# A two-layer graph attention kernel: the cosine threshold made from norms that go through DRAM, without matmuls

## The chip, the core and the metric

The kernel runs on one core of one Trainium2 chip. Its engines each follow a list of instructions in order: TensorE (PE; PEld is its weight load), VectorE (DVE), ScalarE (ACT), GpSimd (POOL) and SyncE (SP, which here only issues DMAs). They meet through semaphores. The metric is the device time of one execution in microseconds (us), the median of several runs; less is better.

## The reference, cut to what matters

128 graphs of 128 nodes with 512 features go through two attention layers. The change touches one line of layer 0: which pairs of nodes have a cosine above 0.1.

```python
def _L0_gnn_ref(embs, score_mask, map_w, map_b, q_w, q_b, k_w, k_b, gcn_map_w, gcn_map_b, gcn_W):
    # embs = relu(layernorm(x)); 8 heads of dk = 64
    m = embs @ map_w.T + map_b
    sem = m.reshape(b, s, h, dk).transpose(0, 2, 1, 3)
    norm = jnp.maximum(jnp.linalg.norm(sem, axis=-1, keepdims=True), COS_EPS)
    n = sem / norm
    cos = jnp.einsum('bhsd,bhtd->bhst', n, n)
    cos = cos * (~sm).astype(cos.dtype)
    cos_adj = (cos > THRESHOLD).astype(embs.dtype)
    q, k = split(m @ q_w.T + q_b), split(m @ k_w.T + k_b)
    scores = jnp.where(sm, NEG, q @ k.T / sqrt(dk))
    p_attn = jax.nn.softmax(scores, axis=-1) * keep
    adj = cos_adj * p_attn
    Ax = adj @ split(embs @ gcn_map_w.T + gcn_map_b)
    return relu((Ax @ gcn_W.T) / (adj.sum(-1, keepdims=True) + 1.0))
# x = x + layer 0; then x = x + layer 1 (softmax attention, 4 heads of 64, masked by adj, output projection)
```

The kernel doesn't divide by the norms. It compares the product of two rows with 0.1 times the product of their norms: m_s . m_t - 0.1 |m_s| |m_t| > 0, for 8 heads of 128x128 pairs in each graph.

## The kernel before, in words

Every product runs on TensorE in float16 with each operand split into an upper and a lower part (`hi`, `lo`; three passes). ACT makes the upper parts (a copy to float16), POOL or DVE the lower ones (original minus upper), and DMA transposes bring them into the layout that the next product needs.

The graphs go through a software pipeline of slots, one for each graph, written out in full. In slot n an engine works on graph n (scores, cosines, softmax and gate of layer 0), on graphs n+1 to n+6 (loads, layer norm, the products m, q, k, v; these for two graphs at once) and on graphs n-1 to n-5 (weighted sums, layer 1, result). **Even and odd slots differ**: q, k and the norms of a pair of graphs are made in odd slots, m and v in even ones. Each engine has its own `slot(s)` function with the calls in the order in which they are issued. Nothing reorders them afterwards; a stage that waits holds up all that stands behind it on its engine. The first slots (preparation of weights, graphs 0 to 2) and the last three (`late_slots`) have orders of their own.

PSUM holds `s_ps` (scores, 2 banks), `c_ps` (cosines, 2 banks) and four banks of `unit_ps` that a table (`UNITS`) gives to products in turn. TensorE may start a unit only when DVE has emptied the last product in that bank. In odd slots bank 3 goes from `o1o` (the sums of layer 1, emptied by `o1_rows(s, 4)`, L1389 and L1391) to `lq` (L1886), and DVE reaches `o1_rows(s, 4)` only after `gate(s)` (L1280).

The threshold before, for a pair of graphs, in the odd slot ahead of them:

1. PE `norms` (L1980) sums the squares; DVE `norm_sums` (L1400) takes them out, times 0.1; POOL `norm_rows` takes the root with a power of 0.5 (L781) and makes float16 upper and lower parts (L786, L788) in `norm_parts`.
2. SP `turn_norms` (L558) transposes them with two DMAs into `norm_t`.
3. DVE `threshold_rows` (L1414) multiplies them by a mask of heads into `norm_r`.
4. PE `cosines` (L1942) adds minus the product of the norms to the cosines in `c_ps`: two matmuls of 64 rows by 512 columns for each graph.

After that `gate` (L1280) keeps those of the exponentials whose `c_ps` is above 0. The exponentials are ACT's (`scores_exp`, L949 and eight L939), the maximum before them DVE's (L1274), the masking DVE's (L1264).

## Time and profile before

| | |
|---|---|
| median of 3 runs | 2512.72 us (2511.32 to 2512.87) |
| profiled execution | 2513.7 us, its span 2511.9 us |
| PE / PEld / DVE / ACT / POOL busy | 99% / 79% / 81% / 69% / 82% |
| granted TensorE clock, mean | 0.997 |
| DMA engines busy | 59.8% (data queue) |

The profile is one execution. "Busy" is the share of the span in which an engine had an instruction running; a matmul's end is modelled. The span leaves out 1.8 us around the program. A wait is shown as idle time in front of an instruction, with the one that released it.

### The profile page before, as it was taken

The numbers are of one execution on the slowest core, as the hardware profiler recorded it, in microseconds if no ns is written. First come the engines' busy times: TensorE is split into PE (matmuls) and PEld (weight loads), VectorE is DVE, ScalarE is ACT, GpSimd is POOL, SyncE is SP. The second block draws the span as 40 slices with busy tenths as digits, with TensorE's granted clock in tenths as the row PEclk, the third lists the DMA queues.
The fourth block names the chain that finished last, engine by engine and source line by source line (L and its number), as shares of the span: only waits on it lengthen the run. The fifth ranks groups of instructions, "written<-read, shape, count | busy, mean of one in ns | idle before, by whom it ended". The sixth has DMA issues, their size and how long they took to land.

```text
span 2511.9 us, 77339 instructions
## 1 busy us (share of the span) xinstructions
PE 2474.3 (99%) x29880; PEld 1978.8 (79%) x29880; DVE 2028.9 (81%) x3426; ACT 1737.7 (69%) x4528; POOL 2064.2 (82%) x2330
## 2 busy tenths in 40 slices
PE   8899999999999999999999999999999999999997
PEld 6677878878878778778788788788787787787775
DVE  6888788788788888888887887888878888888876
ACT  5676676676776766766766766767767667667666
POOL 4788888888888888888888888888888888888875
PEclk9999999999999999999999999999999999999999
DMA  5456665656656656665656566556566666566652
GB/s 154 92 117 120 121 124 115 128 115 124 128 114 123 130 116 118 130 117 120 121 117 126 116 122 127 118 123 128 115 123 129 117 118 126 116 123 121 120 100 75
DMA packets 840557, 300.56 MB, mean 120 GB/s; under 512 B 782464, under 2 KB 790144, under 8 KB 840192
## 3 DMA queue, kind: packets, MB, share of 16 engines
q1 hardware_dynamic: 840192, 295.62, 59.8%
q8 instruction: 238, 3.90, 0.7%
q14 instruction: 127, 1.04, 0.1%
HBM read 75.80 MB, written 33.55 MB: 44 GB/s over the span
## 4 chain that ended last, share of the span: by engine, by line
PE 93%; DVE 2%; ACT 1%; POOL 1%; issue 1%; DMA 1%; SPq 0%; POOLq 0%; DVEq 0%; ACTq 0%
PE unit_ps L1886 26%; PE unit_ps L2064 26%; PE unit_ps L1900 25%; PE s_ps L1910 4%; PE s_ps L1969 4%; PE c_ps L1910 3%; PE unit_ps L2036 2%; PE unit_ps L1910 2%; PE c_ps L1942 1%; PE unit_ps L1980 1%; ACT e_ec L939 0%; DVE e_ec L1280 0%; POOL norm L781 0%; DMA e_ec<-in_L_gnn_q_w_dram 0%; DMA norm_t<-norm_parts 0%
## 5 line engine op out<-in xcount | busy, mean ns | idle before, releaser
L939 ACT ACTIVATE e_ec<-e_ec,neg_mx 128x128 f32<-128x128 f32 x1008 | 390.0, 388 | 4.1
L2064 PE MATMUL unit_ps<-m_hl,w_q_hi 128*128 128x256 f16 x2048 | 358.2, 274 | 0.0
L2064 PE MATMUL unit_ps<-m_hl,w_k_hi 128*128 128x256 f16 x2048 | 355.6, 272 | 0.6 <-DVE qk_sb L1316 0.6
L1035 ACT ACTIVATE qk_hl<-qk_sb 128x512 f16<-128x512 f32 x256 | 153.3, 622 | 283.2 <-DVE qk_sb L1316 283.2
L1886 PE MATMUL unit_ps<-h_t,w_m_hi 128*128 128x256 f16 x2048 | 342.4, 274 | 2.4 <-issue 1.3
L1900 PE MATMUL unit_ps<-w_v_hi,h_t 128*128 128x512 f16 x1024 | 325.1, 379 | 0.0
L996 ACT ACTIVATE h_sb<-x,shift,rstd 128x512 f32<-128x512 f32 x128 | 104.1, 813 | 281.3 <-POOL shift L809 281.3
L1886 PE MATMUL unit_ps<-h_t,w_m_lo 128*128 128x256 f16 x1024 | 280.5, 274 | 0.0
L734 POOL TENSOR_TENSOR e_ec<-e_ec 128x1024 f16<-128x1024 f32 x126 | 269.1, 2136 | 3.3 <-ACT e_ec L969 2.1
L1280 DVE SCALAR_TENSOR_TENSOR e_ec<-c_ps,e_ec 128x1024 f32<-128x1024 f32 x126 | 154.2, 1224 | 118.5 <-ACT e_ec L939 118.5
L2064 PE MATMUL unit_ps<-m_hl,w_q_lo 128*128 128x256 f16 x1024 | 238.6, 273 | 0.0
L2064 PE MATMUL unit_ps<-m_hl,w_k_lo 128*128 128x256 f16 x1024 | 237.3, 272 | 0.0
L2064 PEld LDWEIGHTS unit_ps<-m_hl,w_q_hi 128*128 128x128 f16 x2048 | 200.7, 98 | 39.1 <-issue 16.8
L1886 PEld LDWEIGHTS unit_ps<-h_t,w_m_hi 128*128 128x128 f16 x2048 | 196.0, 98 | 31.9 <-issue 2.8
L2064 PEld LDWEIGHTS unit_ps<-m_hl,w_k_hi 128*128 128x128 f16 x2048 | 200.1, 98 | 23.2 <-issue 0.6
L729 POOL TENSOR_TENSOR p_hl<-p_sb,p_hl 128x512 f16<-128x512 f32 x128 | 148.6, 1161 | 79.9 <-ACT p_hl L962 79.9
L710 POOL TENSOR_TENSOR h_hl<-h_sb,h_hl 128x512 f16<-128x512 f32 x128 | 148.5, 1160 | 67.0 <-ACT h_hl L1004 67.0
L1900 PE MATMUL unit_ps<-w_v_lo,h_t 128*128 128x512 f16 x512 | 194.0, 379 | 0.0
L1900 PEld LDWEIGHTS unit_ps<-w_v_hi,h_t 128*128 128x128 f16 x1024 | 100.2, 98 | 114.1 <-issue 0.3
L1316 DVE SCALAR_TENSOR_TENSOR qk_sb<-unit_ps,qk_factor,col_qb 128x512 f32<-128x512 f32 x128 | 96.1, 751 | 116.2 <-PE unit_ps L2064 115.4
L939 ACT ACTIVATION_READ_ACCUMULATOR e_ec<-e_ec,neg_mx 128x1 f32 x1008 | 188.3, 187 | 0.0
L781 POOL TENSOR_TENSOR norm<-sq_sum,plus_half 128x16 f32<-128x16 f32 x64 | 187.1, 2923 | 1.4 <-DVE sq_sum L1400 1.3
(280 smaller groups left out, 7550.8 us busy)
## 6 DMA issues: line engine op xcount, KB each, us to landing
xa<-in_x_dram SPq DMA_DIRECT2D x128, 256.0 KB, 3.3
x<-in_x_dram SPq DMA_DIRECT2D x128, 256.0 KB, 2.9
out_dram<-x SPq DMA_DIRECT2D x128, 256.0 KB, 2.4
h_t<-h_hl SPq DMA_TRANSPOSE x254, 3.3
ec_t<-e_ec SPq DMA_TRANSPOSE x252, 3.2
adj_in<-in_adj_dram SPq DMA_DIRECT2D x128, 16.0 KB, 2.0
norm_t<-norm_parts SPq DMA_TRANSPOSE x128, 2.3
p_t<-p_hl SPq DMA_TRANSPOSE x126, 3.3
```

The source lines that it names most:

```text
L710: nc.gpsimd.tensor_tensor(h1_hl[:, a, 1, :], h1_sb[:, a, :], h1_hl[:, a, 0, :], ALU.subtract).then_inc(h1_lo, 1)
L729: nc.gpsimd.tensor_tensor(p1_hl[:, b, 1], p1_sb[:, b], p1_hl[:, b, 0], ALU.subtract).then_inc(p1_lo, 1)
L734: nc.gpsimd.tensor_tensor(e_hl[:, 1], e_of(s), e_hl[:, 0], ALU.subtract).then_inc(e_lo, 1)
L781: nc.gpsimd.tensor_tensor(norm[:, :], sq_sum[:, :], plus_half[:, :], ALU.pow).then_inc(norm_done, 1)
L939: ins = nc.scalar.activation(e[:, h, :], e[:, h, :], ACT.Exp, bias=neg[:, h:h + 1], scale=SCALE, accum_out=sums[:, h:h + 1])
L996: nc.scalar.activation(h1_sb[:, a, :], x1[:, (s.n - 1) % 8, :], ACT.Relu, bias=shift1[:, 0:1], scale=rstd1[:, 0:1]).then_inc(h1_done, 1)
L1035: nc.scalar.activation(dst[:, 0, c, :], src[:, c, :], ACT.Copy).then_inc(done, 1)
L1280: nc.vector.scalar_tensor_tensor(out=e_of(s), in0=c_ps[:, :, :].rearrange("p a (b n) -> p (a b) n", b=4), scalar=0.0, in1=e_of(s), op0=ALU ...
L1886: ins = nc.tensor.matmul(out, w[a][:, i, c * P:(c + 1) * P], h[:, :, b, i, :], start=n == 0, stop=n == len(passes) - 1)
L1900: ins = nc.tensor.matmul(ps, h[:, a, i, :], w[b][:, i, :], start=n == 0, stop=n == len(passes) - 1)
L1910: ins = nc.tensor.matmul(outs[half][c], st[r, a, c, cols], mv[r, b, c, cols], start=n == 0 and (last or c == 0), stop=last and n == 2)
L2064: ins = nc.tensor.matmul(ps[:, c % 2 * 2 * P:(c % 2 + 1) * 2 * P], w[a][:, i, c * P:(c + 1) * P], parts[:, b, i, :], start=n == 0, stop=n ...
```

## The change

The threshold is made without TensorE:

- POOL `norm_rows` keeps only the power of 0.5; L786, L788, `norm_parts`, `norm_t`, `norm_r` and the mask are gone.
- SP `keep_norms` stores the norms of both graphs of a pair to DRAM (128 nodes x 2 x 8 float32, pieces of 32 bytes), and `spread_norms`, once that has landed, loads each graph's 128x8 norms into all 128 partitions (`norm_n`, 4 KB in each partition, 512 KB for a graph).
- ACT `threshold` makes `least[s, h, t]` = norm of t (from `norm_n`, read with a step of 8 float32) times 0.1-scaled norm of s (one value for each partition), with eight copies of 128 columns for each graph. `least` has one buffer.
- DVE `above` subtracts `least` from the cosines in PSUM, one operation of 1024 columns for each graph; `gate` waits for it.
- The last graph's `least` is POOL's (`last_threshold`).

```diff
--- before.py
+++ after.py
@@ sync
+            def keep_norms(s):
+                if s.has(1):
+                    sp.wait_ge(norm_done, s.at(lambda t: (t + 1) // 2 + 1))
+                    for g in range(2):
+                        wait(sp, norm_in[g], s.at(lambda t: 16 * ((t + 1) // 2)))
+                    sp.dma_start(norm_d.rearrange("g n h -> n g h"),
+                                 norm[:, :].rearrange("p (g h) -> p g h", g=2)).then_inc(norm_kept, 16)
+            def spread_norms(s):
+                if s.has(1):
+                    wait(sp, threshold_done, s.at(lambda t: t + 1))
+                    sp.wait_ge(norm_kept, s.at(lambda t: 16 * ((t + 1) // 2 + 1)))
+                    for g in range(2):
+                        sp.dma_start(norm_n[:, g].rearrange("p n h -> p (n h)"),
+                                     norm_d[g].rearrange("(a n) h -> a (n h)", a=1).broadcast_to([P, P * H])).then_inc(norm_in[g], 16)
@@ gpsimd, norm_rows
+                    wait(pool, norm_kept, s.at(lambda t: 16 * ((t + 1) // 2)))
+                    wait(pool, threshold_done, s.at(lambda t: t + 1))
                     nc.gpsimd.tensor_tensor(norm[:, :], sq_sum[:, :], plus_half[:, :], ALU.pow).then_inc(norm_done, 1)
-                    ... (copy and subtract into norm_parts)
@@ scalar
+            def threshold(s):
+                if s.has(0):
+                    g = s.n % 2
+                    act.wait_ge(norm_in[g], s.at(lambda t: 16 * (t // 2 + 1)))
+                    act.wait_ge(norm_done, s.at(lambda t: t // 2 + 1))
+                    wait(act, lowered, s.at(lambda t: t))
+                    for h in range(H):
+                        ins = nc.scalar.activation(least[:, h, :], norm_n[:, g, :, h], ACT.Copy, scale=norm[:, g * H + h:g * H + h + 1])
+                    ins.then_inc(threshold_done, 1)
@@ scalar, even slots
+                    threshold(s)
                     scores_exp(s)
@@
                     lv_upper(s)
+                    threshold(Slot(s.n + 1, None, B))
                     h1_rows(s)
@@ vector
+            def above(s):
+                if s.has(0):
+                    dve.wait_ge(c_full, s.at(lambda t: t + 1))
+                    dve.wait_ge(threshold_done, s.at(lambda t: t + 1))
+                    cosine = c_ps[:, :, :].rearrange("p a (b n) -> p (a b) n", b=4)
+                    nc.vector.tensor_tensor(cosine, cosine, least[:, :, :], ALU.subtract).then_inc(lowered, 1)
             def gate(s):
                 if s.has(0):
                     dve.wait_ge(e_done, s.at(lambda t: t + 1))
-                    dve.wait_ge(c_full, s.at(lambda t: t + 1))
+                    dve.wait_ge(lowered, s.at(lambda t: t + 1))
@@ vector, odd slots
                     q_features(s, 0)
                     o1_rows(s, 5)
+                    above(s)
                     q_features(s, 1)
@@
-                    threshold_rows(s)
@@ vector, even slots
                     l1_mask(s, 3)
+                    above(s)
                     gate(s)
@@ tensor, cosines
                     row_pairs([[c_ps[:, a, c * P:(c + 1) * P] for c in range(C)] for a in range(2)], parts, parts,
-                              columns(s.n % 2), last=False)
-                    pe.wait_ge(threshold_done, s.at(lambda t: t // 2 + 1))
-                    for a in range(2):
-                        r = slice(a * DK, (a + 1) * DK)
-                        ins = nc.tensor.matmul(c_ps[:, a, :], norm_t[r, 0, :], norm_r[r, s.n % 2].rearrange("p c n -> p (c n)"),
-                                               start=False, stop=True)
-                    ins.then_inc(c_full, 1)
+                              columns(s.n % 2)).then_inc(c_full, 1)
```

Three places, in the steady part of the program. First ACT, where an even slot begins, before:

```order
L996 ACTIVATE h_sb<-x,shift,rstd 128x512 [waits h1_lo,ln1_step]
L1004 ACTIVATE h_hl<-h_sb 128x512 [waits h1_in,h1_done]
L949 ACTIVATE neg_mx<-mx 128x8 [waits mx_done,den_done]
L939 ACTIVATE e_ec,row_sum<-e_ec,neg_mx 128x128 [waits neg_mx_done]
L939 ACTIVATE e_ec,row_sum<-e_ec,neg_mx 128x128 x7
```

and with the change:

```order
L1007 ACTIVATE h_sb<-x,shift,rstd 128x512 [waits h1_lo,ln1_step]
L1015 ACTIVATE h_hl<-h_sb 128x512 [waits h1_in,h1_done]
L951 ACTIVATE least<-norm_n,norm 128x128 [waits lowered,norm_done,norm_in0]
L951 ACTIVATE least<-norm_n,norm 128x128 x7
L960 ACTIVATE neg_mx<-mx 128x8 [waits mx_done,den_done]
L940 ACTIVATE e_ec,row_sum<-e_ec,neg_mx 128x128 [waits neg_mx_done]
L940 ACTIVATE e_ec,row_sum<-e_ec,neg_mx 128x128 x7
```

The eight products for the even graph stand between layer 1's rows of the slot before (`h_sb`, `h_hl`) and the even graph's exponentials (`e_ec`), and wait for `norm_in0`. Further on in the same even slot, ACT before:

```order
L976 ACTIVATE v_sb<-v_rows_sb 128x8x64 [waits av_full,unit_out1]
L987 ACTIVATE lv_sb<-unit_ps,v_scale 128x8x64 [waits unit_full]
L996 ACTIVATE h_sb<-x,shift,rstd 128x512 [waits h1_lo,ln1_step]
L1004 ACTIVATE h_hl<-h_sb 128x512 [waits h1_in,h1_done]
L976 ACTIVATE v_sb<-v_rows_sb 128x8x64 [waits av_full,unit_out3]
```

and with the change:

```order
L987 ACTIVATE v_sb<-v_rows_sb 128x8x64 [waits av_full,unit_out1]
L998 ACTIVATE lv_sb<-unit_ps,v_scale 128x8x64 [waits unit_full]
L951 ACTIVATE least<-norm_n,norm 128x128 [waits lowered,norm_done,norm_in1]
L951 ACTIVATE least<-norm_n,norm 128x128 x7
L1007 ACTIVATE h_sb<-x,shift,rstd 128x512 [waits h1_lo,ln1_step]
L1015 ACTIVATE h_hl<-h_sb 128x512 [waits h1_in,h1_done]
L987 ACTIVATE v_sb<-v_rows_sb 128x8x64 [waits av_full,unit_out3]
```

The eight products for the odd graph stand behind `lv_sb` and ahead of layer 1's rows, so ahead of the odd graph's exponentials too. Third, SP in an odd slot, before:

```order
L516 DMA_TRANSPOSE o_t<-o_hl 128x4x128 [waits unit_full,o1_lo]
L548 DMA_TRANSPOSE ec_t<-e_ec 128x8x128 [waits av_full,e_hi]
L558 DMA_TRANSPOSE norm_t<-norm_parts 128x1x128 [waits c_full,norm_split]
L558 DMA_TRANSPOSE norm_t<-norm_parts 128x1x128
L548 DMA_TRANSPOSE ec_t<-e_ec 128x8x128 [waits av_full,e_lo]
L584 DMA out_dram<-x 128x512 [waits unit_out3]
```

and with the change:

```order
L516 DMA_TRANSPOSE o_t<-o_hl 128x4x128 [waits unit_full,o1_lo]
L548 DMA_TRANSPOSE ec_t<-e_ec 128x8x128 [waits av_full,e_hi]
L558 DMA norm_d<-norm 128x2x8 [waits norm_in1,norm_in0,norm_done]
L568 DMA norm_n<-norm_d 128x1024 [waits norm_kept,threshold_done]
L568 DMA norm_n<-norm_d 128x1024
L548 DMA_TRANSPOSE ec_t<-e_ec 128x8x128 [waits av_full,e_lo]
L595 DMA out_dram<-x 128x512 [waits unit_out3]
```

One store and two loads of 512 KB stand where two small transposes stood, ahead of the transpose of the lower half of `ec_t`, and SP waits for the store to land (`norm_kept`) in front of the loads.

## Rows read from the trace of the kernel before

**Rows 1.** Page, part 1: busy us (share) and instructions of each engine.
```profile
PE 2474.3 (99%) x29880; PEld 1978.8 (79%) x29880; DVE 2028.9 (81%) x3426; ACT 1737.7 (69%) x4528; POOL 2064.2 (82%) x2330
```

**Rows 2.** Waits, whole run: waiter, releaser, us in total, times, longest us.
```profile
ACT h_sb L996 <- POOL shift L809: 281.3, 127, 3.4
...
DVE e_ec L1280 <- ACT e_ec L939: 118.5, 123, 2.2
...
PE unit_ps L1886 <- DVE o_sb L1391: 0.4, 1, 0.4
```

**Rows 3.** Chain of work, 1206 to 1246: start us, us, what.
```profile
1208.48 0.21 PE c_ps L1942 x2
...
1218.52 2.62 PE unit_ps L1886 x24
```

**Rows 4.** Timeline of ACT, 1199 to 1256: start us, us, instruction, [idle before].
```profile
1208.27 0.81 ACT L996 ACTIVATE h_sb<-x,shift,rstd 128x512 f32<-128x512 f32 x1 [2.00 <-POOL shift L809]
...
1215.94 0.40 ACT L1027 ACTIVATE o_hl<-o_sb 128x256 f16<-128x256 f32 x1
...
1229.25 0.81 ACT L996 ACTIVATE h_sb<-x,shift,rstd 128x512 f32<-128x512 f32 x1 [2.15 <-POOL shift L809]
1230.09 0.63 ACT L1004 ACTIVATE h_hl<-h_sb 128x512 f16<-128x512 f32 x1
1231.98 0.21 ACT L949 ACTIVATE neg_mx<-mx 128x8 f32<-128x8 f32 x1 [1.26 <-DVE mx L1274]
...
1235.54 1.28 ACT L937 ACTIVATE p_sb<-p_sb,neg_lmx 128x128 f32<-128x128 f32 x4
...
1243.24 0.61 ACT L976 ACTIVATE v_sb<-v_rows_sb 128x512 f16<-128x512 f32 x1
1243.76 0.67 ACT L987 ACTIVATE lv_sb<-unit_ps,v_scale 128x512 f16<-128x512 f32 x1
1246.43 0.81 ACT L996 ACTIVATE h_sb<-x,shift,rstd 128x512 f32<-128x512 f32 x1 [2.00 <-POOL shift L809]
```

**Rows 5.** Timeline of POOL, the same stretch.
```profile
1206.21 0.23 POOL L805 TENSOR_SCALAR nm<-mv 128x1 f32<-128x1 f32 x1
...
1218.16 2.90 POOL L781 TENSOR_TENSOR norm<-sq_sum,plus_half 128x16 f32<-128x16 f32 x1
...
1222.03 1.15 POOL L755 TENSOR_TENSOR qk_hl<-qk_sb,qk_hl 128x512 f16<-128x512 f32 x1
...
1227.18 1.09 POOL L805 TENSOR_SCALAR nm<-mv 128x1 f32<-128x1 f32 x1
```

**Rows 6.** Timeline of DVE, the same stretch.
```profile
1214.51 0.75 DVE L1316 SCALAR_TENSOR_TENSOR qk_sb<-unit_ps,qk_factor,col_qb 128x512 f32<-128x512 f32 x1 [1.69 <-PE unit_ps L2064]
1216.06 1.22 DVE L1280 SCALAR_TENSOR_TENSOR e_ec<-c_ps,e_ec 128x1024 f32<-128x1024 f32 x1 [0.80 <-ACT e_ec L939]
...
1217.41 0.42 DVE L1391 TENSOR_TENSOR o_sb<-unit_ps,inv_lsum 128x256 f32<-128x256 f32 x1
...
1226.98 1.21 DVE L1414 TENSOR_TENSOR norm_r<-norm_t,norm_mask 128x1024 f16<-128x1024 f16 x1
```

**Rows 7.** DMA issues: times, KB each, median us from issue to landing.
```profile
x<-in_x_dram SPq DMA_DIRECT2D x128, 256.0 KB, 2.9
...
norm_t<-norm_parts SPq DMA_TRANSPOSE x128, 2.3
...
p_sb<-in_L_gnn_Wv_dram SPq DMA_DIRECT2D x1, 512.0 KB, 7.2
bias_o<-in_L_gnn_bo_dram SPq DMA_DIRECT2D x1, 256.0 KB, 7.3
```

**Rows 8.** Stretches: busy us by engine, PEclk, DMA share, GB/s (last).
```profile
24.00:28.00 4.00, 3.99 (x34) 3.64 (x35) 4.00 (x8) 4.00 (x6) 0.00 (x0) 1.00 1.08 338
...
1222.00:1230.00 8.00, 8.00 (x122) 6.44 (x120) 6.15 (x7) 2.07 (x3) 7.51 (x9) 1.00 0.30 59
```

**Rows 9.** Timeline of ACT, first slot.
```profile
62.40 0.19 ACT L949 ACTIVATE neg_mx<-mx 128x8 f32<-128x8 f32 x1
```

More of the change, by code:

```diff
@@ L282, in build @@
         ec_t = sb("ec_t", [P, 2, H, P], F16)
-        norm_parts = sb("norm_parts", [P, P + 2 * H], F16)
-        norm_t = sb("norm_t", [P, 2, P], F16)
-        norm_r = sb("norm_r", [P, 2, C, P], F16)
-        norm_mask = sb("norm_mask", [P, 2 * C])
+        norm_d = nc.dram_tensor("norm_d", (2, P, H), F32).ap()
+        norm_n = sb("norm_n", [P, 2, P, H])
+        least = sb("least", [P, H, P])
         ident16 = sb("ident16", [P, P], F16)
@@ L395, in build @@
         norm_done = sem("norm_done")
-        norm_split = sem("norm_split")
-        norm_in = sem("norm_in")
+        norm_kept = sem("norm_kept")
+        norm_in = [sem(f"norm_in{i}") for i in range(2)]
         threshold_done = sem("threshold_done")
+        lowered = sem("lowered")
         masked = sem("masked")
@@ L643, in _ @@
             turn_e(z, 0, e_hi)
-            turn_norms(z)
+            keep_norms(z)
+            spread_norms(z)
             turn_e(z, 1, e_lo)
@@ L1092, in slot @@
                     squares(s)
+                    threshold(s)
                     scores_exp(s)
@@ L1095, in slot @@
                     v_upper(s, "va", 2)
+                    threshold(Slot(s.n + 1, None, B))
                     h1_rows(s)
@@ L1099, in slot @@
                 else:
+                    threshold(s)
                     scores_exp(s)
@@ L1107, in slot @@
                     lv_upper(s)
+                    threshold(Slot(s.n + 1, None, B))
                     h1_rows(s)
@@ L1202, in _ @@
             lqk_upper(z, "lq", lq_hl, LQ)
+            threshold(a)
             scores_exp(a)
@@ L1535, in slot @@
                     l1_mask(s, 3)
+                    above(s)
                     gate(s)
@@ L1756, in _ @@
             o1_rows(z, 5)
+            above(z)
             q_features(z, 1)
@@ L1766, in _ @@
             x1_stats(z)
-            threshold_rows(z)
             lqk_lower(z, "lq", lq_hl, LQ, 0)
             scores_mask(a)
+            above(a)
             scores_mask(b)
@@ L1774, in _ @@
             x1_stats(a)
+            above(b)
             gate(b)
@@ L1902, in rows, with row_pairs @@
                 return ins
-            def row_pairs(outs, mv, st, cols, last=True):
+            def row_pairs(outs, mv, st, cols):
                 for c in range(len(outs[0])):
@@ L1910, in row_pairs @@
                             ins = nc.tensor.matmul(outs[half][c], st[r, a, c, cols], mv[r, b, c, cols],
-                                                   start=n == 0 and (last or c == 0), stop=last and n == 2)
+                                                   start=n == 0, stop=n == 2)
                 return ins
@@ L1977, in norms @@
                     for g in range(2):
-                        out = ps[:, 0:2 * H].rearrange("p (a g c) -> p g a c", a=2, g=2)[:, g]
+                        out = ps[:, 0:2 * H].rearrange("p (g a c) -> p g a c", a=2, g=2)[:, g]
                         for n, (c, part) in enumerate((c, part) for c in range(C) for part in range(2)):
```

53 lines of the change are left out of this document (13 added, 40 removed).

## The prediction

> **What bounds the kernel now.** I read the page's busy shares first. TensorE is busy 99% of the span, but the other four are at 69% to 82% [rows 1], so one engine made slower could take over. Then the waits of the whole run: TensorE hardly waits for anyone. The longest that bears on the change is ACT, which waits 281 us in all for POOL's layer norm of layer 1, and DVE's gate waits 118 us for ACT's exponentials [rows 2]. Those waits are slack, and the question is who uses it up. Last the chain of work and the timelines of one pair of graphs (an odd and an even slot). Layer 1's rows in ACT (L996) start at 1208.27 and again at 1246.43: a pair takes 38.16 us [rows 4]. There are 64 pairs, and about 61 of them run at this pace; the first and last 70 to 110 us are different.
>
> **TensorE.** The two threshold matmuls of a graph are 0.21 us of the chain [rows 3], since both halves of the array run at once (the groups show 0.38 us for each matmul, but they overlap). Two graphs: 0.43 us a pair, so TensorE alone would need 37.73 us. Over 61 pairs that is -26 us. Nothing else in TensorE changes.
>
> **Where a delay would reach TensorE.** In odd slots unit `lq` starts at 1218.52 in the bank that `o1_rows(s, 4)` empties; that ends at 1217.41 + 0.42 = 1217.83 and stands behind the gate, which starts when the odd graph's exponentials are done [rows 3, 6]. So 0.7 us less the semaphore, about 0.5 us, is all that the odd exponentials may be late against TensorE. Only one such wait is in the trace, of 0.4 us [rows 2].
>
> **The round through ACT and POOL.** The odd exponentials end (L1027 starts) at 1215.94; then POOL's power at 1218.16, its `q` lower part at 1222.03, the rest of POOL's slot up to shift L809, which releases ACT's L996 at 1229.25, L1004, exponentials from 1231.98, the ACT work up to L987, L996 at 1246.43, and the next odd exponentials [rows 4, 5]. I step through it with the change:
>
> - POOL loses L786 and L788: the power ends at 1221.06, and the lower part of `q`, which started at 1222.03, follows at 1221.10. -0.93 us.
> - POOL's L805 took 1.09 us, from 1227.18 to 1228.27, beside L1414 of DVE, from 1226.98 to 1228.19 [rows 5, 6]. The same operation with no such neighbour takes 0.23 us [rows 5], so I count L1414's going as -0.86 us. Bounds: 0 (something else takes its place) and -1.2 us (L804 before it goes faster too). The two make 1.79 us, ACT's L996 starts at 1227.46, and ACT is free 0.84 + 0.54 us later, at 1228.84.
> - The even graph's eight products. No ACT copy of 128 columns stands in the trace. The nearest is L937, 128 columns with one value per partition, contiguous: four in 1.28 us with the first 0.39, so 0.297 us for each further one [rows 4]. Eight: 2.38 us. Bounds: below, no less than this pitch, since a shape as short is mostly fixed cost; above, 0.40 each, if every column takes twice the 0.82 ns that I get from 0.61 us for 512 and 0.39 us for 128 less their fixed part: 3.2 us. I take 2.38. ACT is done at 1231.22, and the even exponentials start there instead of 1231.98: 0.76 us early, as the maximum (DVE, relieved of L1414) is ready by then.
> - From L949 to the end of L987 nothing changes. L987 starts 1243.76 and its follower could have started 0.09 before its end (as 1243.24 + 0.61 and 1243.76 show), at 1244.34 [rows 4]. Early by 0.76: 1243.58. The odd graph's products: 2.38, so 1245.96, where L996 had waited until 1246.43 for POOL. 0.47 us early; what was 2.00 us of idle is full.
>
> So the round would take 38.16 - 0.47 = 37.69 us, and TensorE 37.73 us. **They tie.** The cover that hides 4.8 us of new ACT work a pair is spent to the last tenth; any shift of POOL's or ACT's pieces (the bounds above are -0.3 to +0.9 us on the POOL side) shows in the time if it is late and not if it is early. I put 0.15 us a pair on that: +9 us over 61 pairs.
>
> **DVE.** L1414 goes (1.21 us in this pair); two subtractions come. The gate has their shape and operands (1024 columns, one operand in PSUM, one in SBUF): 1.22 us [rows 6]. Plus 1.2 us a pair, and both lie in waits: in odd slots ahead of `q_features(s, 1)`, where DVE sat 1.69 us for TensorE; in even slots ahead of the gate, where it sits for ACT's exponentials (118.5 us over 123 times, 1 us each [rows 2]). Cost 0; if the cover is gone, 0.2 us for a graph in even slots (1.2 against 1.0).
>
> **SP and DMA.** The store can go when the power ends, 1221.06. No store of 32-byte pieces is in the trace; the nearest small transfer lands after 2.3 us [rows 7]. Bounds 2 and 5 us. Then 512 KB: 256 KB of x land after 2.9 us, and another 256 KB at the 338 GB/s of the weight loads is 0.8 us [rows 7, 8]: 3.7. Together with issue the even graph's norms are there at about 1227.4, and ACT wants them at 1228.84. That the source is the same 4 KB for all partitions costs nothing that I can see: the broadcast bias took 7.3 us where its neighbour in the queue took 7.2 [rows 7]. The engines are 30% busy from 1222 to 1230 [rows 8], so there is room. The lower half of `ec_t`, now behind 1 MB, lands near 1231 instead of 1229; TensorE needs it at 1235. Cost 0.
>
> **Ends of the program.** In slot 0 ACT is the chain: its exponentials start at 62.40 straight behind other work [rows 9]; the first eight products go in front of them, +2.4 us, and those of graph 1 stand in front of graph 1's; DVE's L1414 is gone there. I take +4 us (0 to 5). At the end the norms were on the chain already; a store and a load (6 us) take the place of two POOL operations, a transpose and L1414 (about 7), against two subtractions and POOL's last product: +1 us.
>
> **The sum** against the profiled execution: -26 + 9 + 4 + 1 = -12 us, span 2511.9 to 2500, execution 2513.7 to 2501.5. The median of the runs is 1 us under the profiled one: 2500.5 us.
>
> **Rivals.** *The strided read.* `threshold` reads `norm_n` with a step of 32 bytes, and no ACT operation of the trace reads SBUF with such a step. If each column then takes twice as long, eight products take 3.2 us: +0.84 twice a pair. The round is 39.4 us, TensorE waits for bank 3 in every odd slot, and 1.2 us over 61 pairs is +74, +10 at the ends with 8 more products there: 2597 us. This is the case on the other side. For it: the step is new. Against: short operations are mostly fixed cost. 0.27.
>
> The Trainium skill ("SBUF — State Buffer", section "Door 1: The DMA port swizzle (why `[64,N]` ≈ `[32,N]`)") speaks for this rival: engines read 16-byte lines, and "how far you can stride for free depends on dtype: 4 fp32"; here the step is 8. No row of this case shows it.
>
> *Norms late.* If the store takes 5 us and the load 4, ACT has the even norms at 1230.1 at best, 1.3 us after it is free: round 39.0 us, +0.8 us a pair against before, +49 and +5 at the ends: 2567 us. For it: 256 pieces of 32 bytes, at a time when the queue is full up to 1222. Against: the small rows of [rows 7]. 0.13. The Trainium skill ("DMA: Bandwidth & Descriptors", section "Specifications") has pieces under 512 bytes done as read-modify-write, which would lengthen this store; no run here shows it.
>
> *All hidden.* POOL gains the whole 1.2 us, the round is shorter than TensorE's 37.73, and the gain is -26 + 3: 2490 us. 0.14.
>
> **Chances.** The forecast 0.46, its own range 2488 to 2525 us (0.33 of it under 2507.7, 0.08 within 5 us of before, 0.05 above). About 0.2%, 5 us, is what a measurement tells from no change. Faster 0.14 + 0.33 = 0.47, same 0.08, slower 0.05 + 0.27 + 0.13 = 0.45. The range that leaves out 2 in 10 runs from the all-hidden case to about the middle of the strided one: 2487 to 2598.
>
> **What would show it.** ACT's products at 0.30 us apart (0.40: the strided rival). Their first one in even slots with no wait for a DMA (a wait for `norm_n`: norms late). ACT's 281 us wait for POOL nearly gone; POOL's L805 back at 0.23. TensorE waiting for `o_sb` in front of `lq`, in few pairs and for tenths, if they tie; in each pair for over 0.5 us, if I am wrong on the round. A pair at 37.7 to 37.9 us. The forecast falls if TensorE waits elsewhere, as for `ec_t` or the end of the cosines.

## The result and the profile after

The changed kernel takes 2642.38 us (median of 4 runs, 2641.85 to 2643.54) against 2512.23 us before: ratio 1.0515, 95% interval 1.0502 to 1.0529. It is 130 us slower, where I forecast 12 us faster, and 44 us above the end of my range. The profiled span went from 2511.9 to 2640.8 us.

Page, part 1, of the changed kernel (busy us, share, instructions; before: [rows 1]):

```profile
PE 2484.8 (94%) x29624; PEld 1981.5 (75%) x29624; DVE 2131.1 (81%) x3490; ACT 2147.2 (81%) x5544; POOL 1981.2 (75%) x2195
```

TensorE's busy time grew by 10 us though 256 matmuls are gone (part of the run is at a lower granted clock, below); its share fell to 94%. ACT grew by 410 us. The chain of work that ended last (page, part 4), by engine, first before and then with the change:

```profile
PE 93%; DVE 2%; ACT 1%; POOL 1%; issue 1%; DMA 1%; SPq 0%; POOLq 0%; DVEq 0%; ACTq 0%
```

```profile
ACT 53%; issue 21%; POOL 15%; PE 8%; DVE 2%; DMA 1%; ACTq 0%; SPq 0%; POOLq 0%; DVEq 0%
```

TensorE was the bound and is no longer. The waits of the whole run answer to [rows 2] (waiter, releaser, us, times, longest):

```profile
DVE e_ec L1305 <- ACT e_ec L940: 235.7, 109, 3.5
...
PE unit_ps L1903 <- DVE o_sb L1416: 105.4, 60, 2.1
...
ACT h_sb L1007 <- POOL shift L809: 57.1, 49, 3.0
```

ACT no longer waits for POOL for 281 us. The gate waits twice as long for ACT, and TensorE now waits in nearly every pair for the bank that `o1_rows(s, 4)` empties behind the gate (L1903 is what L1886 was, L1416 what L1391 was, L1007 what L996 was). The timeline of ACT, one pair (answers to [rows 4]; from the L1007 of one odd slot to that of the next 39.96 us, where 38.16 stood from one even slot to the next):

```profile
1293.53 0.81 ACT L1007 ACTIVATE h_sb<-x,shift,rstd 128x512 f32<-128x512 f32 x1 [1.08 <-POOL shift L809]
1294.38 0.63 ACT L1015 ACTIVATE h_hl<-h_sb 128x512 f16<-128x512 f32 x1
1294.91 3.45 ACT L951 ACTIVATE least<-norm_n,norm 128x128 f32<-128x128 f32 x8
1298.27 0.19 ACT L960 ACTIVATE neg_mx<-mx 128x8 f32<-128x8 f32 x1
...
1310.04 0.67 ACT L998 ACTIVATE lv_sb<-unit_ps,v_scale 128x512 f16<-128x512 f32 x1
1310.61 3.44 ACT L951 ACTIVATE least<-norm_n,norm 128x128 f32<-128x128 f32 x8
1313.95 0.80 ACT L1007 ACTIVATE h_sb<-x,shift,rstd 128x512 f32<-128x512 f32 x1
...
1321.61 0.40 ACT L1038 ACTIVATE o_hl<-o_sb 128x256 f16<-128x256 f32 x1
...
1333.49 0.82 ACT L1007 ACTIVATE h_sb<-x,shift,rstd 128x512 f32<-128x512 f32 x1 [1.09 <-POOL shift L809]
```

Both blocks of eight stand without a gap in front and behind: ACT is full from 1293.53 to 1321.61. A block holds ACT for 3.36 us (from 1294.91 to 1298.27) or 3.34 us (from 1310.61 to 1313.95), and I had 2.38. The groups (busy us, mean ns, idle before):

```profile
L951 ACT ACTIVATE least<-norm_n,norm 128x128 f32<-128x128 f32 x1016 | 437.9, 515 | 3.0 <-DMA norm_n<-norm_d 3.0
```

A product takes 0.515 us and starts 0.42 us after the last one (from 3.45 - 0.51 over 7). Its idle time for a DMA is 3.0 us in the whole run, once.

POOL in the odd slot (answers to [rows 5]) and TensorE at the bank:

```profile
1323.83 2.90 POOL L782 TENSOR_TENSOR norm<-sq_sum,plus_half 128x16 f32<-128x16 f32 x1
1326.71 1.15 POOL L754 TENSOR_TENSOR qk_hl<-qk_sb,qk_hl 128x512 f16<-128x512 f32 x1
1327.82 2.57 POOL L733 TENSOR_TENSOR e_ec<-e_ec 128x1024 f16<-128x1024 f32 x1
...
1332.30 0.23 POOL L805 TENSOR_SCALAR nm<-mv 128x1 f32<-128x1 f32 x1
```

```profile
1323.65 0.38 PE L1903 MATMUL unit_ps<-h_t,w_lq_hi 128*128 128x256 f16 x2 [2.07 <-DVE o_sb L1416]
```

L805 is at 0.23 us as forecast, but that shows little: before, it took about 1.1 us in only 14 of its 128 executions, and one of them was the pair that I had read. The lower half of `e_ec` (L733), 2.13 us in the same stretch before, takes 2.57; before it had the row

```profile
1223.15 2.13 POOL L734 TENSOR_TENSOR e_ec<-e_ec 128x1024 f16<-128x1024 f32 x1
```

The starts of L1007 over the whole run give the pairs: of 60 steady ones 44 take about 39.95 us and 16 about 40.43, mean 40.08 (before 37.9 to 38.5, mean 38.15). 60 x 1.93 = 116 us; the first and last slots are 13 us longer. That is the 129 us of the span.

### The profile page after: what moved, and what is told of

Its sections match the earlier page's. It is cut to its first block, busy times and chain, and to the rows that moved or that the text cites. A ratio compares the mean times of both kernels' runs of the same rounds, so it can differ in the third digit from the quotient of the medians.

```text
span 2640.8 us, 78086 instructions
## 1 busy us (share of the span) xinstructions
PE 2484.8 (94%) x29624; PEld 1981.5 (75%) x29624; DVE 2131.1 (81%) x3490; ACT 2147.2 (81%) x5544; POOL 1981.2 (75%) x2195
## 4 chain that ended last, share of the span: by engine, by line
ACT 53%; issue 21%; POOL 15%; PE 8%; DVE 2%; DMA 1%; ACTq 0%; SPq 0%; POOLq 0%; DVEq 0%
ACT least L951 15%; ACT e_ec L940 13%; PE unit_ps L1903 5%; ACT p_sb L938 5%; POOL e_ec L733 4%; POOL qk_hl L754 4%; ACT h_sb L1007 4%; ACT v_sb L987 3%; ACT e_ec L980 2%; ACT m_hl L1064 2%; POOL x L715 2%; PE unit_ps L2075 2%; ACT h_hl L1027 2%; ACT xa L1022 2%; ACT sq_hl L1054 2%
## 5 line engine op out<-in xcount | busy, mean ns | idle before, releaser
L951 ACT ACTIVATE least<-norm_n,norm 128x128 f32<-128x128 f32 x1016 | 437.9, 515 | 3.0 <-DMA norm_n<-norm_d 3.0
L1903 PE MATMUL unit_ps<-h_t,w_m_hi 128*128 128x256 f16 x2048 | 341.2, 274 | 4.1 <-DVE qk_sb L1341 3.1
L733 POOL TENSOR_TENSOR e_ec<-e_ec 128x1024 f16<-128x1024 f32 x126 | 296.6, 2354 | 11.4 <-ACT e_ec L980 8.8
L1903 PE MATMUL unit_ps<-h_t,w_lq_hi 128*128 128x256 f16 x1024 | 197.0, 297 | 106.5 <-DVE o_sb L1416 105.4
L1903 PE MATMUL unit_ps<-h_t,w_m_lo 128*128 128x256 f16 x1024 | 279.9, 273 | 0.0
L1903 PEld LDWEIGHTS unit_ps<-h_t,w_m_hi 128*128 128x128 f16 x2048 | 195.8, 98 | 33.0 <-issue 4.4
L1365 DVE TENSOR_TENSOR qk_hl<-qk_sb,qk_hl 128x512 f16<-128x512 f32 x128 | 180.6, 1411 | 45.8 <-ACT qk_hl L1046 45.8
L1903 PEld LDWEIGHTS unit_ps<-h_t,w_lq_hi 128*128 128x128 f16 x1024 | 104.9, 106 | 140.8 <-issue 120.5
```

What stands on the lines that cost most here:

```text
L733: nc.gpsimd.tensor_tensor(e_hl[:, 1], e_of(s), e_hl[:, 0], ALU.subtract).then_inc(e_lo, 1)
L951: ins = nc.scalar.activation(least[:, h, :], norm_n[:, g, :, h], ACT.Copy, scale=norm[:, g * H + h:g * H + h + 1])
L1365: nc.vector.tensor_tensor(k_hl[:, 1, c, :], k_sb[:, c, :], k_hl[:, 0, c, :], ALU.subtract).then_inc(k_lo, 1)
L1903: ins = nc.tensor.matmul(out, w[a][:, i, c * P:(c + 1) * P], h[:, :, b, i, :], start=n == 0, stop=n == len(passes) - 1)
```

## The experiments

Each stands against runs of the kernel before on the same chip. The cuts of code are shortened (`...`). "Pair" is the distance of L1007 (L996) from one odd slot to the next, the commonest value of the profiled execution.

### e1: the products read contiguously

```diff
-ins = nc.scalar.activation(least[:, h, :], norm_n[:, g, :, h], ACT.Copy, scale=...)
+ins = nc.scalar.activation(least[:, h, :], norm_n[:, g].rearrange("p n h -> p (n h)")[:, h * P:(h + 1) * P], ACT.Copy, scale=...)
```

> The changed kernel, but ScalarE's products read 128 contiguous values of norm_n instead of every eighth one (so they take the norms of the wrong nodes; everything else, the store and the loads too, is as in the changed kernel). Theory A, the step: a product took 0.42 us from one to the next (3.36 us for eight) because of the 32-byte step; contiguous it takes the 0.30 us of the exponentials of 128 columns, eight take 2.4 us, the round through ScalarE and GpSimd is 2 us a pair shorter, and the time is 2510 to 2525 us. Theory B, the products themselves or the DMA traffic beside them are slow (a copy with one factor per partition, 1 MB of loads per pair): the pitch stays near 0.42 us and the time near 2640 us.

Measured: 2505.93 us, ratio to before 0.9972 (0.9961 to 0.9984), pair 37.93 us.

```profile
L951 ACT ACTIVATE least<-norm_n,norm 128x128 f32<-128x128 f32 x1016 | 309.0, 387 | 3.0 <-DMA norm_n<-norm_d 3.0
```

The same operation takes 515 ns in the changed kernel and 387 here, with the same loads running beside it; eight take 2.43 us. Theory A holds: 136 us hang on the step of one read. It came out below my 2510 to 2525, 5 us above the 2500.5 us of the forecast.

### e2, e5, e3: the step in between, with a layout that is right

The norms are stored and spread in blocks of W heads: W = 4 (step of 16 bytes, e2), 2 (8 bytes, e5), 1 (contiguous, e3).

```diff
-norm_n = sb("norm_n", [P, 2, P, H])
+norm_n = sb("norm_n", [P, 2, H // W, P, W])
-sp.dma_start(norm_d.rearrange("g n h -> n g h"), ...)
+sp.dma_start(norm_d.rearrange("g c n w -> n (g c) w"), ...)
-nc.scalar.activation(least[:, h, :], norm_n[:, g, :, h], ...)
+nc.scalar.activation(least[:, h, :], norm_n[:, g, h // W, :, h % W], ...)
```

> The changed kernel with the norms stored and spread as 2 blocks of 4 heads: pieces of 16 bytes in the store, ScalarE reads norm_n with a step of 16 bytes. It computes the same as the changed kernel. Theory A as the Trainium skill has it (page 'SBUF — State Buffer', a step of 4 float32 is free): pitch 0.30 us, as contiguous, 2510 to 2525 us. If the cost grows with the step: pitch between 0.30 and 0.42, about 0.36 us, eight take 2.9 us and the time is about 2575 us. Theory B: 0.42 us and 2640 us. If the 512 pieces of the store land later than the 128 to 256 of before, ScalarE waits for norm_n.

> The changed kernel with the norms stored and spread as 4 blocks of 2 heads: ScalarE reads norm_n with a step of 8 bytes; the store has 1024 pieces of 8 bytes. It computes the same as the changed kernel. Steps of 16 and of 32 bytes gave the same pitch of 0.42 us for 128 columns and a step of 4 bytes 0.30 us. If any step but the contiguous one costs this, the pitch is 0.42 us again and the store on top makes ScalarE wait for norm_n (the 2048 pieces of 4 bytes landed too late by 7.6 us a pair): 2700 us or more. If a step of 8 bytes is still free, the pitch is 0.30 us. The pitch is what this run is for; its time depends on the store.

> The changed kernel with the norms stored head by head: pieces of 4 bytes, 2048 of them in the store, and a contiguous read in ScalarE. It computes the same as the changed kernel. Theory A: pitch 0.30 us, and if the store lands in under about 5 us, 2510 to 2525 us; if the small pieces take longer (8 us or more), ScalarE waits for norm_n in even slots for 3 us or more a pair and the time is 2600 us or above. Theory B: pitch 0.42 us, 2640 us.

Measured: e2 2644.47 us (ratio 1.0524, 1.0508 to 1.0540), e5 2598.02 (1.0345, 1.0331 to 1.0359), e3 2955.52 (1.1765, 1.1745 to 1.1786). The groups of e2, e5, e3:

```profile
L951 ACT ACTIVATE least<-norm_n,norm 128x128 f32<-128x128 f32 x1016 | 437.2, 515 | 3.3 <-DMA norm_n<-norm_d 3.1
```

```profile
L951 ACT ACTIVATE least<-norm_n,norm 128x128 f32<-128x128 f32 x1016 | 319.0, 398 | 80.4 <-DMA norm_n<-norm_d 80.4
```

```profile
L951 ACT ACTIVATE least<-norm_n,norm 128x128 f32<-128x128 f32 x1016 | 309.7, 388 | 441.6 <-DMA norm_n<-norm_d 441.6
```

16 bytes cost exactly what 32 do; e2's time is the one that I had named for theory B, but e1 has ruled that theory out. 8 bytes are nearly free (398 against 387 ns). The price has moved into the store: its rows (times, KB, median us to landing) in the changed kernel, e2 and e5 are

```profile
norm_d<-norm SPq DMA_DIRECT2D x64, 8.0 KB, 1.9
```

```profile
norm_d<-norm SPq DMA_DIRECT2D x64, 8.0 KB, 2.8
```

```profile
norm_d<-norm SPq DMA_DIRECT2D x64, 8.0 KB, 4.7
```

for the same 8 KB in 256, 512 and 1024 pieces; with 2048 pieces ACT waited 441.6 us for the loads behind it. With 32-byte pieces the store lands just under my range of 2 to 5 us. The Trainium skill (page "DMA: Bandwidth & Descriptors", section "Specifications"), cited in the prediction for read-modify-write under 512 bytes, let me expect a longer store; at 1.9 us, under the 2.3 us that I took, none shows. No run has pieces of 512 bytes or more to compare.

### e4: one product instead of eight

```diff
-for h in range(H):
+for h in range(1):
     ins = nc.scalar.activation(least[:, h, :], ...)
```

The other seven heads' parts of `least` are set to 0 once, at the start.

> The changed kernel with one product of 128 columns for each graph instead of eight (the other seven heads keep a threshold of 0); all waits, the store, the loads and the subtraction stay. If ScalarE's time is the whole loss and nothing else of the change costs: the round through ScalarE and GpSimd is 2 x 2.9 = 5.9 us shorter than in the changed kernel, TensorE is the bound at 37.73 us a pair and the time is 2488 to 2495 us. If DMA (waits for norm_n, a late ec_t) or VectorE's subtraction costs something of its own, it is above 2500 us.

Measured: 2485.54 us (ratio 0.9891, 0.9876 to 0.9905), pair 37.70 us, 2.5 us below the range I gave. The loads, the store, the waits and the subtraction, all still there, cost nothing as long as TensorE is the bound. TensorE alone needs 37.70 us a pair; the prediction had 37.73.

### e6: contiguous for the even graph alone

```diff
+norm_n[:, g, :, h] if g else norm_n[:, g].rearrange("p n h -> p (n h)")[:, h * P:(h + 1) * P]
```

> The changed kernel, ScalarE's products contiguous for the even graph of a pair alone (with the norms of the wrong nodes), strided for the odd one. If both blocks of eight stand on one round whose pieces add up: half of what the contiguous read gave, less what lies below TensorE's own pace: the changed kernel takes about 40.1 us a pair, so this one 39.1 us, and 2575 to 2585 us. If only one of the two blocks is on the path, the time is near 2506 or near 2642 us.

Measured: 2569.15 us (1.0222, 1.0207 to 1.0238), a little under 2575. Pairs: 37.93 (e1), 38.93 (e6), 39.95 us (changed kernel). Each block of eight adds 1.0 us, which is 3.45 - 2.43 = 1.02 of the block itself. Both blocks are on one round, and it adds.

### e10: one POOL operation out of the round

```diff
@@ gpsimd, odd slots
                     e_lower(s)
-                    result_base(s)
                     norm_l1(s)
+                    result_base(s)
```

> The changed kernel with one move: in odd slots GpSimd makes layer 1's layer norm (norm_l1) ahead of result_base (L715, 1.27 us), which stood in front of it. It computes the same. If the round odd exponentials - GpSimd - ScalarE L1007 - exponentials is the bound: up to 1.3 us of it go, but ScalarE reaches L1007 only after the lk part (L1072), which TensorE's late lq holds: in the trace of the changed kernel that leaves 0 to 1.1 us a pair, on the mean about 0.5: 2600 to 2620 us. If the round is not what bounds it: 2642 us.

Measured: 2575.03 us (1.0239, 1.0225 to 1.0253), pair 38.76 us: 67 us faster with the strided read in place. More than expected: I had read ACT's slack from a pair of 40.43 us, in which L1007 does not wait for POOL; in most pairs it waits 1.1 us. So the round through POOL was the bound, and nearly all of L715's 1.27 us came back (39.95 - 38.76 = 1.2 us). What holds e10 at 38.76 us, still 1 us above TensorE's pace, is a second round (see e14 and e17).

### e15: e1's contiguous read and e10's move together

> The contiguous read (the norms of the wrong nodes, as in e1) with result_base behind norm_l1. The round is 36.9 us, TensorE bounds at 37.73: 2483 to 2490 us, against 2506 of e1. If the 20 us that e1 lay above the run with one product came from somewhere else than the round (DMA, VectorE's subtraction): 2506 us stays.

Measured: 2491.32 us (0.9920, 0.9906 to 0.9935), pair 37.70: TensorE's own pace. The 15 us between this and e1 are the tie that the forecast priced at 9 us (0.15 a pair; it was 0.23).

### e7, e9: what the matmuls are worth in the kernel before

e7 cuts the threshold matmuls to 8 columns, e9 the product with the mask too (both leave the threshold out for all other columns):

```diff
@@ e7 and e9, tensor
-nc.tensor.matmul(c_ps[:, a, :], norm_t[r, 0, :], norm_r[r, s.n % 2].rearrange("p c n -> p (c n)"), ...)
+nc.tensor.matmul(c_ps[:, a, 0:8], norm_t[r, 0, :], norm_r[r, s.n % 2].rearrange("p c n -> p (c n)")[:, 0:8], ...)
@@ e9, vector, threshold_rows
-nc.vector.tensor_tensor(norm_r[:, :, :, :]...)
+nc.vector.tensor_tensor(norm_r[:, :, 0, 0:8], ...)
```

> The kernel before, with its two threshold matmuls of a graph (L1942) cut from 512 to 8 columns; norms, transposes, the products with the mask and all waits stay (the threshold is left out for all but 8 columns). My step: 0.21 us a graph of TensorE's chain, 0.43 us a pair, -26 us: 2486 to 2489 us, since before these the round through ScalarE and GpSimd had 2 us of slack. If TensorE was not the bound or the round is as long: 2505 us or more.

> The kernel before with eight columns in its threshold matmuls (L1942), as the run before, and with the product with the mask (L1414) cut to the same eight columns (the threshold is left out for all others). Theory P: TensorE lost 0.28 us a pair in the run before because layer 1's scores (L1910) wait for the lower part of lk (L1365), which stands behind L1414 on VectorE, and lq for the gate; without L1414 the wait for lk is gone, and the time is 2486 to 2495 us. Theory Q: another bound (the round through GpSimd with L786 and L788, or the clock) holds the kernel at 2506 us whatever L1414 takes.

Measured: e7 2506.28 us (0.9974, 0.9963 to 0.9985), pair 38.00; e9 2485.82 (0.9887, 0.9873 to 0.9900), pair 37.74. The matmuls alone give 6 us, not 26. The timeline of VectorE in e7 shows who held TensorE:

```profile
1259.59 2.29 DVE L1414 TENSOR_TENSOR norm_r<-norm_t,norm_mask 128x1024 f16<-128x1024 f16 x1
1261.80 0.74 DVE L1365 SCALAR_TENSOR_TENSOR lk_hl<-unit_ps,unscale,lk_hl 128x512 f16<-128x512 f32 x1
```

and its chain of work at the same place:

```profile
1261.80 0.75 DVE lk_hl L1365
1262.55 0.05 issue
1262.59 0.84 PE unit_ps L1910 x24
```

L1414 stands in front of L1365, and layer 1's scores (L1910) need L1365. It is so in the whole run: in 62 of 64 pairs of e7 L1910 starts 0.06 us after L1365 ends. This was the next bound behind the matmuls, and with L1414 gone too (e9, theory P) the time is about 20 us less. The change takes both away, so the sum of the prediction (-26) was right for the change and its account was not. L786 and L788, which e9 keeps, were worth nothing there.

The trace of the kernel before had already shown how near this bound was:

```profile
PEld unit_ps L1910 <- DVE lk_hl L1365: 4.0, 12, 0.9
```

In 12 of 64 pairs the weight loads of L1910 waited for L1365, and over all pairs L1910 started only 0.24 us (median) after L1365's end. Of the 0.43 us a pair that the matmuls take, less than 0.2 could be gained.

### e8, e16: products and subtraction as one VectorE operation

```diff
-    nc.vector.tensor_tensor(cosine, cosine, least[:, :, :], ALU.subtract)
+    for h in range(H):
+        nc.vector.scalar_tensor_tensor(out=cosine_h, in0=norm_n[:, g, :, h], scalar=norm_s_h, in1=cosine_h, op0=ALU.mult, op1=ALU.subtract)
```

e16 reads `norm_n` contiguously (the norms of the wrong nodes). ACT has no products in either, and the gate tests for below 0.

> The changed kernel with ScalarE's products and VectorE's subtraction made one: eight VectorE operations of 128 columns a graph (norm of t times norm of s minus the cosine, into PSUM), and the gate tests for below 0; `least` is gone. It computes the same. If an operation of 128 columns takes 0.19 us from one to the next (the 256-column and 512-column ones go by 0.34 and 0.65 us), the eight take 1.5 us against 1.1 us of the subtraction: the even graph's gate is about 0.5 us late, ScalarE is as free as before, and TensorE is the bound: 2485 to 2495 us, faster than both kernels. If VectorE pays for the 32-byte step as ScalarE did (0.3 us each, 2.6 us a graph): gates late by 1.6 us, what hangs on them on GpSimd too, 2500 to 2560 us.

> The fused run (VectorE multiplies and subtracts, eight operations of 128 columns) with a contiguous read of norm_n (the norms of the wrong nodes). Strided, the operations went 0.36 us apart. If VectorE pays for the 32-byte step: about 0.22 us apart, 1.1 us a graph less, and 2695 us falls to 2560 to 2600 us. If VectorE's cost is in small operations whatever their step: 0.36 us and 2695 us.

Measured: e8 2695.14 us (1.0727, 1.0712 to 1.0742), e16 2518.55 (1.0026, 1.0014 to 1.0038). An operation of each, first e8 and then e16:

```profile
1239.87 2.91 DVE L1275 SCALAR_TENSOR_TENSOR c_ps<-norm_n,norm,c_ps 128x128 f32<-128x128 f32 x8
```

```profile
1237.89 2.15 DVE L1275 SCALAR_TENSOR_TENSOR c_ps<-norm_n,norm,c_ps 128x128 f32<-128x128 f32 x8
```

VectorE pays for the step too (0.35 against 0.26 us from one to the next). Both are dearer than my 0.19 us, taken from operations with 256 and 512 columns and no strided or broadcast operand. The step alone, 1.5 us of operations a pair, is worth 177 us of time, 2.9 us a pair: TensorE waits 111 us for VectorE in e8 and 20 in e16, and its mean granted clock is 0.965 against 0.996. How the rest divides stays open. Both expectations missed: e8 is 135 us above the highest time that I gave, e16 41 us below its range.

### e11, e12: a cheap step by a store for each graph

```diff
-keep_norms(s)
-spread_norms(s)
-turn_e(s, 1, e_lo)
+keep_norms(s, 0)        # 4 blocks of 2 heads
+spread_norms(s, 0)
+keep_norms(s, 1)
+turn_e(s, 1, e_lo)
+spread_norms(s, 1)
```

> The changed kernel with the norms of each graph stored and loaded by themselves as 4 blocks of 2 heads (512 pieces of 8 bytes a graph, read by ScalarE with a step of 8 bytes), the even graph's first, the odd graph's load behind the transpose of the lower half of ec_t. It computes the same as the changed kernel. The products go 0.30 us apart, as with one store of 1024 pieces; that store landed after 4.7 us and ScalarE waited 1.3 us a pair for it, one of 512 pieces should land after about 2.8 us (as 512 pieces of 16 bytes did), within the 1.5 us or so that the contiguous version had left: 2503 to 2512 us, as the contiguous read. If the smaller store still comes late: 2530 to 2560 us.

> The run before this one, and result_base behind norm_l1 on GpSimd in odd slots. It computes the same. In the contiguous version ScalarE's L1007 waited 1.1 us for GpSimd's shift in odd slots; with the 1.27 us out of the way the round is about 36.9 us a pair, below TensorE's 37.73: 2484 to 2492 us, faster than both kernels. If the result of the slot (L1475 on VectorE), which needs result_base, then comes late, or another wait follows, 2495 us or more.

Measured: 2609.32 us (1.0378, 1.0364 to 1.0392) and 2617.80 (1.0411, 1.0396 to 1.0425); both expectations missed. From the DMA issues and the waits of e11:

```profile
norm_d<-norm SPq DMA_DIRECT2D x128, 4.0 KB, 4.1
```

```profile
PE unit_ps L1920 <- DMA o_t<-o_hl: 86.5, 57, 4.2
...
ACT least L954 <- DMA norm_n<-norm_d: 60.8, 51, 5.0
```

512 pieces of 8 bytes take 4.1 us, not the 2.8 of 512 pieces of 16. And SP, which waits for two stores in turn, comes late to the transpose of `o_t` at the head of its next slot: a new wait for TensorE. SP's wait for the stores was 101.6 us in the changed kernel and is

```profile
SPq L565 <- DMA norm_d<-norm: 463.8, 125, 5.4
```

in e11. The products are cheap with the 8-byte step (398 ns), but the way to it through DMA costs more than it gives back. In e12 ACT's wait for `norm_n` grew to 84.9 us, and the move on POOL gained nothing.

### e14, e13, e17, e18: keep the step, move a block to POOL

The even graph's products become one POOL operation of 1024 columns behind `h1_lower` (e14); with `result_base` behind `norm_l1` (e13); with `result_base` of odd slots moved up behind `x_lower` (e17). e18 makes that last move in the kernel before.

```diff
@@ gpsimd, even slots (e14, e13, e17)
                     h1_lower(s)
+                    threshold(s)      # tensor_tensor of 128x1024, norm_n strided, norm broadcast
@@ scalar, even slots
-                    threshold(s)
                     scores_exp(s)
@@ gpsimd, odd slots (e17, e18)
                     x_lower(s)
+                    result_base(s)
                     o1_lower(s, 5)
@@ gpsimd, odd slots, further on (e17, e18)
                     e_lower(s)
-                    result_base(s)
                     norm_l1(s)
```

> The same with the even graph's products on GpSimd, but result_base where it was: the round is 11.9 + 18.4 + 7.7 = 38.0 us a pair, 0.3 us above TensorE's: 2500 to 2512 us. If the round is not the bound it is the same as with both moves.

> The changed kernel with its layout and the strided read, with two moves: the even graph's products are one GpSimd operation of 1024 columns (as the last graph's, 2.43 us) behind h1_lower in even slots, and result_base stands behind norm_l1 in odd slots. It computes the same. From the traces: odd exponentials to L1007 10.7 us (run e10), L1007 to L1007 in the even slot 1.38 + 1.35 for the maximum + 11.8 + 0.6 + 3.3 = 18.4 us on ScalarE (on GpSimd 17.2 + 1.1 = 18.3), L1007 to the end of the odd exponentials 7.7 us: 36.8 us, below TensorE's 37.73: 2484 to 2495 us. If GpSimd, with 2.4 us more, or the subtraction that waits for it makes another wait: 2500 us or more.

> The changed kernel, strided read and layout as they are, with the even graph's products as one GpSimd operation behind h1_lower, and result_base of odd slots (L715, 1.27 us) moved up to behind x_lower, where GpSimd sat idle for 1.86 us until ScalarE's o_hl. It computes the same. Behind norm_l1 (e13) it delayed the result, the mask and the maximum, for which ScalarE then waited 3.0 us a pair; here it is early. The round was 38.46 us in e14; 1.2 us of it go: 37.3 us, below TensorE's 37.73: 2484 to 2495 us, faster than both kernels. If result_base delays o1_lower or q_lower by more than the idle time covers, or the clock or another wait takes over: 2500 us or more.

> The kernel before with result_base of odd slots moved up in the same way and nothing else. It computes the same. TensorE is its bound (38.16 us a pair, 99% busy) and ScalarE had 2 us to spare in the round: no change, 2510 to 2515 us. If it is faster by over 5 us, the gain of the run with both moves is not the change's.

Measured: e14 2540.32 us (1.0112, 1.0097 to 1.0128), pair 38.47; e13 2546.20 (1.0133, 1.0116 to 1.0150), 38.53; e17 2543.15 (1.0112, 1.0097 to 1.0128), 38.47; e18 2512.52 (0.9997, 0.9989 to 1.0006). The waits of e17 show why the move gave nothing this time:

```profile
ACT neg_mx L971 <- DVE mx L1300: 160.3, 61, 2.7
...
PE unit_ps L1911 <- DVE o_sb L1424: 37.5, 60, 2.0
```

ACT waits no more for POOL but for VectorE's maximum. In its timeline the odd exponentials end at 1234.07 and `neg_mx` starts at 1248.88: 14.81 us through `o1_rows(4)`, TensorE's lq, k and lk, their parts on ACT and VectorE, the result, the mask and the maximum. From `neg_mx` ACT is full for 12.65 us to the odd graph's block (1261.53), which takes 3.34, and then 7.66 to the end of the odd exponentials (1272.53): 38.46 us. In e14 it is the same (14.82 us from 1230.98 to 1245.80), so that POOL's layer norm was no longer on the round there. A second round leads through ACT's block for the odd graph, over VectorE and TensorE. The chain of e17 has it, from the odd exponentials' end over `o1_rows(4)` to lq, k and lk in a row:

```profile
1235.54 0.43 DVE o_sb L1424
...
1236.11 2.78 PE unit_ps L1911 x24
1238.89 2.62 PE unit_ps L2083 x24
1241.51 2.62 PE unit_ps L1911 x24
```

With the block at 2.4 us this round would be 37.5 us (an estimate), under TensorE's pace; e15, with contiguous blocks, does run at that pace. My expectations priced only the first round, and took 18.4 us for ACT's even slot where it is 18.9 in e14; for e14 they were 28 us too low, for e13 and e17 about 50. In e13 the move traded one wait of ACT for another: it waits 9.0 us for POOL's layer norm and 182.5 for the maximum, against 74.1 and 88.4 in e14. e18 came out as expected: in the kernel before the move is worth nothing.

No version with the reference's thresholds for all heads beat the kernel before; the best was e14, 1.1% slower.

## Why the prediction was wrong, by its own steps

- **The step that failed: the price of a product.** "The nearest is L937, ... contiguous: ... 2.38 us. Bounds: ... above, 0.40 each". It measured 3.36 us for eight, 0.42 each, above my upper bound; contiguous (e1) it was the 2.4 us that I took, so the step of the read is what failed the term. I had named the step of 32 bytes and given it 0.27, and took the duration of a contiguous neighbour because it was the only row of 128 columns. The weight on that rival should have been larger: its operand was the one thing about the operation that no row covered.
- **The bound of it.** I let each column cost twice its 0.82 ns. It rose by 0.13 us over 128 columns, 1.0 ns each (515 - 387 ns), which makes 2.2 times. The 0.82 ns doesn't follow from the two durations named with it: from 0.39 us for 128 columns to 0.61 for 512 is 0.57 ns a column, and the upper bound would have been 0.37 us each. Rows of the kernel before from 512 to 1024 columns (L1004 0.63 us, L1053 1.04 us) do give 0.80 ns. With 2 x (3.36 - 2.38) = 2.0 us on a round of 37.69, the pair is 39.65 us; that is 92 of the 130 us against before, and 108 against the forecast pair of 37.88.
- **The round.** Right in kind and in place: ACT's 281 us of waiting went, TensorE waits for `o_sb` in front of lq, in 60 pairs. That the round and TensorE tie was nearly exact: 37.93 us in e1, where I had 37.88. Some luck is in it, as the next two points show.
- **POOL's gain.** Forecast -0.93 - 0.86 = -1.79 us from the end of the odd exponentials to L1007; it is 11.87 or 11.88 us against 13.31 before [rows 4], -1.43 (mean of 61 pairs: 11.98 against 13.48). L733 gave up 0.44 (2.57 for 2.13): before, it had started ahead of VectorE's lower part (L1340) in 60 odd slots and kept its 2.13 us; with the change that lower part (L1365) has started first in 62, and 0.59 us of L733 lie beside it. In e10 L805 meets L1365 alone and takes 0.57 us for 0.23. The 0.86 us for L805 was read from an untypical pair: in most pairs L1414, which takes 1.95 us in the mean and not the 1.21 of [rows 6], lay mostly beside L716 and L804. L716 (L715 with the change), L804 and L805 together took 2.96 us before and 1.92 after, so the size was about right by luck. In all 0.36 us a pair is missing; e10 shows that such time counts in full.
- **TensorE's -26 us.** Right for the change, by a wrong account: e7 gives 6 us, e9 28. The two matmuls hid most of the wait behind L1414, but the trace of before had 12 such waits, and I overlooked them.
- **DMA and DVE at nothing.** Right. The store landed in 1.9 us (2.3 taken), the loads in 4.9 (3.7 taken, too low), ACT waited once, for 3.0 us; e4 shows that neither they nor the subtraction cost anything where TensorE is the bound. "Norms late" fell here, and came true in e3, e5 and e11, with smaller pieces.
- **Ends.** +5 forecast, +13 measured. In e1 they are +4, so about 9 us are the strided read's too.
- **The clock.** Not foreseen. About every fourth pair takes 40.43 us. The stretches of such a pair (us, busy by engine, PEclk, DMA share, GB/s):

```profile
1241.00:1243.30 2.30, 0.23 (x3) 0.06 (x2) 1.92 (x5) 2.30 (x6) 1.60 (x2) 1.00 1.02 197
1243.30:1245.00 1.70, 1.70 (x12) 1.35 (x13) 1.63 (x6) 0.67 (x2) 1.70 (x2) 0.71 0.97 328
1245.00:1248.00 3.00, 3.00 (x19) 2.21 (x18) 2.96 (x5) 0.88 (x2) 3.00 (x3) 0.60 1.35 95
1248.00:1252.00 4.00, 4.00 (x39) 3.59 (x37) 1.70 (x4) 1.07 (x2) 3.75 (x5) 1.00 0.61 119
```

TensorE waited 2.07 us for the bank, and then its granted clock was 0.71 and 0.60 over 4.7 us, part of it at the lower level of 1.2 GHz. The 24 matmuls of lq, 2.62 us before [rows 3], have this row in the chain:

```profile
1243.27 4.45 PE unit_ps L1903 x24
```

16 such pairs at 0.48 us are 8 us. In e1, where TensorE waits 2.1 us for that bank in the whole run, all pairs but two take 37.9 us, and TensorE is busy 2457.2 us where it is 2484.8 in the changed kernel with the same matmuls.

The chances were 0.47 faster and 0.45 slower, so the direction was a coin toss, and the 2642 us are the strided rival (2597 us) plus 17 us for the products (3.36 against 3.22), 22 for POOL's part and 8 for the clock, within 2 us (the 3 us that the ends took beyond the rival's 10 are not in this sum).

## What to carry to other kernels

A new operand pattern has no price until a row shows it: where an operation is added with a stride, a broadcast or a piece size that the trace doesn't have, give its rival at least the chance of the forecast, above all where the cover is spent to the last tenth. When a round is found, add the new work on it and look for a second round through the same engine: here one went over POOL and one over TensorE and VectorE. And ask what becomes late when work is removed: matmuls of 26 us were worth 6 as long as one VectorE operation stood right behind them. Last, look at an operation over the whole run before its duration in one pair goes into a sum.
